# Three layer norms inside their layers' blocks, and a first group of keys stacked in two halves

## The reference

```python
x = x + attn(_layernorm(x))     # L0 bond attention, L1 selective scan, L2 dual attention, L3 plain attention
x = x + ffn(_layernorm(x))      # L0 masked, L1 experts, L2 ternary weights, L3 int8 weights

# L1 ffn: softmax over 128 logits, arg max chooses one of 8 experts, its output times the probability
# L2 ffn
h = silu((x @ w1.T) * s1) * ((x @ w2.T) * s2)
h = gelu((h @ h1.T) * sh1); h = gelu((h @ h2.T) * sh2)
out = (h @ w3.T) * s3
# L3 ffn, weights int32 times 1/127
out = (silu(x @ wg.T) * (x @ wu.T)) @ wd.T
# L2 attn (its dense half) and L3 attn: 16 heads of 8
out = softmax(q @ k.T * scale) @ v
```

## Time and profile before

| | us |
|---|---|
| median of three executions | 3002.31 |
| lowest, highest | 2993.35, 3003.5 |
| profiled execution | 3001.56 |
| its span, first to last instruction | 2999.8 |
| mean granted clock of TensorE | 0.906 of full |
| busy PE, ACT, DVE, POOL | 2391.6, 2010.3, 1861.0, 1070.1 |
| DMA, share of 16 engines | 16.3% |

### The profile page before, as it was taken

The page is one execution under the profiler, slowest core; times in us unless marked ns, Lnnn a source line. Parts: engine busy times, 40 slices in busy tenths (PEclk is TensorE's granted clock), DMA queues, the critical chain, the costliest instruction groups (busy, mean ns, idle before and its releaser), DMA issues. The chain is left out here.

```text
span 2999.8 us, 33172 instructions
## 1 busy us (share of the span) xinstructions
PE 2391.6 (80%) x12604; PEld 834.6 (28%) x12604; DVE 1861.0 (62%) x2715; ACT 2010.3 (67%) x2036; POOL 1070.1 (36%) x408
## 2 busy tenths in 40 slices
PE   3677787767666666767999889998679679999995
PEld 1122222334222222333222332223434412222223
DVE  5788888857999999865899438995330401102114
ACT  3999999813633333334999759996332379999991
POOL 4999999611099999431002200031000000000000
PEclk8899999978888898878999999999879879999997
DMA  2012211110154444103111100001010220210000
GB/s 74 1 43 59 69 43 43 43 53 8 29 182 160 168 159 156 58 13 82 30 26 21 41 1 11 11 3 45 7 40 0 53 46 17 42 30 14 15 7 27
DMA packets 66705, 144.64 MB, mean 48 GB/s; under 512 B 15115, under 2 KB 29799, under 8 KB 65832
## 3 DMA queue, kind: packets, MB, share of 16 engines
q1 hardware_dynamic: 66536, 142.40, 16.3%
HBM read 117.92 MB, written 24.25 MB: 47 GB/s over the span
## 5 line engine op out<-in xcount | busy, mean ns | idle before, releaser
L602 POOL TENSOR_TENSOR l0a_diff_pool<-l0a_A,l0a_a_of_t 128x2048 f32<-128x2048 f32 x128 | 531.7, 4192 | 36.3 <-ACT l0a_a_of_t L617 35.8
L1829 ACT ACTIVATE l2x_pT<-ps 128x1024 f32<-128x1024 f32 x512 | 495.8, 1021 | 13.2 <-PE ps L1788 11.3
L1829 ACT ACTIVATE l3he_pT<-ps 128x1024 f32<-128x1024 f32 x512 | 496.0, 1021 | 9.9 <-PE ps L1788 8.1
L1190 PE MATMUL ps<-l1s_hc,all_ident 128*128 128x512 f32 x512 | 285.1, 710 | 155.1 <-POOL l1s_hc L1161 100.7
L585 DVE SCALAR_TENSOR_TENSOR l0a_diff_dve<-l0a_A,l0a_pos,ps 128x512 f32<-128x512 f32 x512 | 345.0, 743 | 30.4 <-PE ps L460 30.4
L1152 POOL TENSOR_TENSOR l1s_dBx<-l1a_dtx,l1a_Bs 128x1024 f32<-128x1024 f32 x128 | 297.4, 2352 | 112.1 <-POOLq L886 112.1
L1176 ACT ACTIVATE ps<-l1a_dt,l1a_A 128x1024 f32<-128x1024 f32 x128 | 143.1, 1118 | 267.9 <-DVE l1s_hc L1235 215.7
L1788 PE MATMUL ps<-l3h_Qs,l3h_Ks 75*128 75x512 bf16 x1024 | 271.1, 389 | 24.7 <-DVE ps L1877 24.7
L1788 PE MATMUL ps<-l2m_Qs,l2m_Ks 75*128 75x512 bf16 x1024 | 273.5, 392 | 9.8 <-PEq L2111 9.8
L1802 PE MATMUL ps<-l2x_pT,l2m_Va 128*9 128x512 f32 x2048 | 271.6, 603 | 1.2 <-ACT l2x_pT L1829 1.2
L1802 PE MATMUL ps<-l3he_pT,l3h_Va 128*9 128x512 f32 x2048 | 270.9, 602 | 0.6 <-ACT l3he_pT L1829 0.6
(11 more groups left out here) (443 smaller groups left out, 3357.2 us busy)
## 6 DMA issues: line engine op xcount, KB each, us to landing
l1a_Bs<-l1a_bc SPq DMA_DIRECT2D x64, 512.0 KB, 3.6
l1s_Cs<-l1a_bc SPq DMA_DIRECT2D x64, 512.0 KB, 4.7
l0a_band_rows<-l0a_band SPq DMA_DIRECT2D x32, 512.0 KB, 5.3
l0a_band<-l0a_exps SPq DMA_DIRECT2D x16, 512.0 KB, 5.1
l2m_Ks<-l2m_parts SPq DMA_DIRECT2D x36, 128.0 KB
l2m_Qs<-l2m_parts SPq DMA_DIRECT2D x72, 64.0 KB
l3h_Ks<-l3h_parts SPq DMA_DIRECT2D x36, 128.0 KB
l3h_Qs<-l3h_parts SPq DMA_DIRECT2D x72, 64.0 KB
```

Source lines behind the costliest of these rows:

```text
L602: pool.tensor_tensor(out, window(s), atb[:, p % 2, :].unsqueeze(1).broadcast_to([P, 4, CH]), ALU.subtract).then_inc(diff_pool, 1)
L1190: mm = pe.matmul(g.ps[:, (4 + 2 * h + q) * CH:(5 + 2 * h + q) * CH], g.ident[:, :], hc[:, m % NHC, q * CH:(q + 1) * CH], start=(n == 0), s ...
L1829: act.activation(pT[:, turn % NPT, :], g.ps[:, slot * QC:(slot + 1) * QC], ACT.Exp).then_inc(expd, 1)
```

## The change

Three layer norms (ln3, ln5, ln7) become objects of a new class `LayerNorm`, whose parts are called at the head of each engine's list in the layer's own block; the block of their own is gone. PE transposes into banks 4 to 7. ACT copies quarter 0 after its fifth block and not after its eighth. SP no longer waits for the loads; PE (ln3, ln5) and DVE (ln5, ln7) do. Of DVE's six steps after the root three become two, so that five remain. In ln5 the four scale vectors are loaded as 16 rows of 128, transposed by PE in one instruction and copied by DVE, and PE waits for that copy before the second product. In ln7 DVE turns the weights into floats while ACT takes the root.

In `head_prepare` ACT's order becomes: squares and copies of k0, k1; squares of k2, k3; copies of q0, q1; squares of q0 to q3; copies of k2, k3; the root; copies of q2, q3. DVE splits k0, k1, q0, q1, k2, then the guard, then k3, q2, q3. SP stores k0 and k1 and, with early True, stacks the first 1024 columns of k after these two; then q0, q1, stacks q, stores k2, the guard, k3, q2, q3. The late half of the first group's keys is stacked at the start of the heads' block on a semaphore of its own, for which PE waits before the ninth key tile of the first segment. The small products of the norm's maximum go to bank 0 instead of banks 2 and 3.

```diff
+    def sync(self, sp):
+        self.n = self.load(sp, self.loads)
+    def tensor(self, pe):
+        for b in range(TB):
+            pe.wait_ge(self.norm[b % 2], b // 2 + 1)
+            mm = pe.transpose(self.g.ps[:, self.at + b * P:self.at + (b + 1) * P], self.xn[:, b, :], self.g.ident[:, :])
+            if b % 4 == 3:
+                mm.then_inc(self.turned, 1)
+    def copy(self, eng, fn, q):
+        eng.wait_ge(self.turned, q + 1)
+        fn(self.g.hT[:, q * CH:(q + 1) * CH], self.g.ps[:, self.at + q * CH:self.at + (q + 1) * CH]).then_inc(self.copied[q % 2], 1)
+    def scalar(self, act):
+        act.wait_ge(self.var_ready, 1)
+        act.activation(self.sd[:, :], self.ve[:, :], ACT.Sqrt).then_inc(self.std_ready, 1)
+        act.wait_ge(self.scale_ready, 1)
+        for b in range(1, TB, 2):
+            act.activation(self.xn[:, b, :], self.g.X[:, b, :], ACT.Identity, bias=self.nm[:, b:b + 1], scale=self.rs[:, b:b + 1]).then_inc(self.norm[1], 1)
+            if b == 9:
+                self.copy(act, act.copy, 0)
+        self.copy(act, act.copy, 2)
+    def vector(self, dve, meanwhile=None):
+        step = Steps(dve, self.steps)
+        ve, sd, rs, tmp = self.ve, self.sd, self.rs, self.tmp
+        for b in range(TB):
+            last = dve.bn_stats(self.st[:, b, :], self.g.X[:, b, :])
+        step(last)
+        for b in range(TB):
+            last = dve.bn_aggr(self.mv[:, b, :], self.st[:, b, :])
+        step(last)
+        dve.tensor_scalar(ve[:, :], self.mv[:, :, 1], 1.0e-5, None, ALU.add).then_inc(self.var_ready, 1)
+        if meanwhile is not None:
+            meanwhile()
+        dve.wait_ge(self.var_ready, 1)
+        dve.wait_ge(self.std_ready, 1)
+        step(dve.reciprocal(rs[:, :], sd[:, :]))
+        step(dve.tensor_tensor(tmp[:, :], rs[:, :], rs[:, :], ALU.mult))
+        step(dve.scalar_tensor_tensor(tmp[:, :], tmp[:, :], -0.5, ve[:, :], ALU.mult, ALU.mult))
+        step(dve.scalar_tensor_tensor(rs[:, :], tmp[:, :], 1.5, rs[:, :], ALU.add, ALU.mult))
+        dve.scalar_tensor_tensor(self.nm[:, :], self.mv[:, :, 0], -1.0, rs[:, :], ALU.mult, ALU.mult).then_inc(self.scale_ready, 1)
+        for b in range(0, TB, 2):
+            dve.tensor_scalar(self.xn[:, b, :], self.g.X[:, b, :], self.mv[:, b, 0:1], rs[:, b:b + 1], ALU.subtract, ALU.mult).then_inc(self.norm[0], 1)
+        for q in range(1, NCH, 2):
+            self.copy(dve, dve.tensor_copy, q)
...
-        layernorm_transpose(nc, g, "ln3", load)
+        ln = LayerNorm(nc, g, ctx, "ln3", load, 4)
...
+            @block.sync
+            def _(sp):
+                ln.sync(sp)
...
             def _(pe):
+                ln.tensor(pe)
+                ln.loaded(pe)
 
                 def logits(q):
+                    ln.quarter(pe, q)
...
                 def experts(b):
                     if b >= 2:
                         pe.wait_ge(zrd[b % 2], b // 2)
+                    else:
+                        for q in range(2 * b + 2):
+                            ln.quarter(pe, q)
...
             def _(act):
...
             @block.vector
             def _(dve):
+                ln.vector(dve)
...
-    def stack_k(sp, hg, slot, sem):
...
-        rows_of(sp, 1, hg, Ks[:, slot, :, :], slice(0, T), sem)
...
+    def stack_k(sp, hg, slot, sem, cols=slice(0, T)):
...
+        rows_of(sp, 1, hg, Ks[:, slot, :, cols], cols, sem)
...
-        if not early:
+        if early:
+            stack_k(sp, 0, 0, hd.k_late, slice(T // 2, T))
...
+        COPIED = (0, 1, NCH, NCH + 1, 2, 3, NCH + 2, NCH + 3)
...
+        def copied(m):
+            return 2 * (COPIED.index(m) + 1)
...
+        def was_split(m):
+            return COPIED.index(m) + 1
...
 
                 def norms(n, at):
                     pe.wait_ge(squared, NCH * (n + 1))
-                    pe.wait_ge(qcp, 2 * (at + 1))
+                    pe.wait_ge(qcp, copied(at))
...
-                pe.wait_ge(qcp, 2 * 3)
-                pe.matmul(g.ps[0:1, 2 * CH:2 * CH + P], km[:, 0:1], g.ident[:, :], start=True, stop=True).then_inc(krow, 1)
+                pe.matmul(g.ps[0:1, 0:P], km[:, 0:1], g.ident[:, :], start=True, stop=True).then_inc(krow, 1)
...
-                pe.wait_ge(qcp, 2 * 4)
-                pe.matmul(g.ps[:, 3 * CH:3 * CH + 1], kr[:, 1:5, :].rearrange("a c s -> a (c s)"), g.ones[0:1, 0:1], start=True, stop=True).then_inc(kcol, 1)
+                pe.matmul(g.ps[:, 0:1], kr[:, 1:5, :].rearrange("a c s -> a (c s)"), g.ones[0:1, 0:1], start=True, stop=True).then_inc(kcol, 1)
                 norms(1, 1)
                 pe.wait_ge(qcp, 2 * HALF)
...
-                pe.matmul(g.ps[0:1, 2 * CH:2 * CH + P], km[:, 2:3], g.ident[:, :], start=True, stop=True).then_inc(urow, 1)
+                pe.matmul(g.ps[0:1, 0:P], km[:, 2:3], g.ident[:, :], start=True, stop=True).then_inc(urow, 1)
...
-                    if m >= NCH:
+                    if m == NCH:
                         act.wait_ge(nps, 1)
...
-                for m in range(NCH + 2):
+                for m in (0, 1):
                     square(m)
                     copies(m)
-                for m in (NCH + 2, NCH + 3):
+                for m in (2, 3):
                     square(m)
-                for m in (NCH + 2, NCH + 3):
+                for m in (NCH, NCH + 1):
+                    copies(m)
+                for m in range(NCH, HALF):
+                    square(m)
+                for m in (2, 3):
                     copies(m)
                 act.wait_ge(nps, 2)
                 act.wait_ge(kcd, 1)
                 act.activation(mT[:, :], bank(1), ACT.Sqrt, scale=km[:, 1:2]).then_inc(und, 1)
+                for m in (NCH + 2, NCH + 3):
+                    copies(m)
...
-                for m in range(NCH):
+                for m in (0, 1, NCH):
                     parts_of(m)
                 dve.wait_ge(nps, 1)
                 dve.tensor_reduce(km[:, 0:1], bank(0), AX, ALU.max).then_inc(kmd, 1)
-                parts_of(NCH)
+                parts_of(NCH + 1)
...
-                parts_of(NCH + 1)
...
+                dve.tensor_copy(km[:, 1:2], g.ps[:, 0:1]).then_inc(kcd, 1)
+                parts_of(2)
                 dve.wait_ge(und, 1)
...
                 dve.wait_ge(urow, 1)
...
+                parts_of(3)
...
                 def store(m, stored):
                     i, q = which(m)
-                    sp.wait_ge(split, m + 1)
+                    sp.wait_ge(split, was_split(m))
                     sp.dma_start(parts[i, :, :, q * CH:(q + 1) * CH].rearrange("a p t -> p a t"), pt[:, m, :, :]).then_inc(stored, 16)
-                for m in range(NCH):
-                    store(m, k_stored)
+                for m in (0, 1):
+                    store(m, k_stored[0])
...
-                    sp.wait_ge(k_stored, 16 * NCH)
-                    stack_k(sp, 0, 0, k_in[0])
+                    sp.wait_ge(k_stored[0], 32)
+                    stack_k(sp, 0, 0, k_in[0], slice(0, T // 2))
                 for m in (NCH, NCH + 1):
                     store(m, q_stored[0])
...
+                store(2, k_stored[1])
                 store_guard(sp, gsplit, gstored)
                 if early:
                     stack_guard(sp, 0, 0, q_in[0])
+                store(3, k_stored[1])
...
-                sp.wait_ge(k_stored, 16 * NCH)
-                sp.wait_ge(q_stored[0], 32)
-                sp.wait_ge(q_stored[1], 32)
+                for half in range(2):
+                    sp.wait_ge(k_stored[half], 32)
+                    sp.wait_ge(q_stored[half], 32)
...
+    if n == TB // 2 and j == 0 and hd.k_late is not None:
+        pe.wait_ge(hd.k_late, hd.KIN)
...
-                sp.dma_start(sc[:, i, :], I[f"L2_ffn_{nm}_s"].rearrange("(k p) -> p k", p=P), allow_slow_non_contiguous=True).then_inc(s, 16)
+                sp.dma_start(scr[K * i:K * (i + 1), :], I[f"L2_ffn_{nm}_s"].rearrange("(k p) -> k p", p=P)).then_inc(s, 16)
...
-        layernorm_transpose(nc, g, "ln5", load)
+        ln = LayerNorm(nc, g, ctx, "ln5", load, 4)
...
+                ln.tensor(pe)
+                ln.loaded(pe)
+                pe.transpose(g.ps[:, 3 * CH:3 * CH + 4 * K], scr[:, :], g.ident[0:4 * K, 0:4 * K]).then_inc(sct, 1)
                 for n in range(N1):
                     m, q = n % K, n // K
+                    if m == 0:
+                        ln.quarter(pe, q)
+                    if n == 1:
+                        pe.wait_ge(scc, 1)
...
+                ln.scalar(act)
+                act.wait_ge(scc, 1)
...
+                ln.vector(dve)
+                dve.wait_ge(sct, 1)
+                dve.tensor_copy(sc[:, :, :].rearrange("p i k -> p (i k)"), g.ps[:, 3 * CH:3 * CH + 4 * K]).then_inc(scc, 1)
+                dve.wait_ge(scc, 1)
+                ln.loaded(dve)
...
+                    if m == 0:
+                        ln.quarter(pe, q)
...
-                dve.tensor_scalar(w[:, :, :], wi[:, :, :], SCALE, None, ALU.mult).then_inc(deq, 1)
```

(7 more changed lines are left out.)

42 lines of the change are left out of this document (36 added, 6 removed).

## The result

The changed kernel takes 2982.17 us (median of five, 2980.09 to 2986.45) against 2999.01 for the kernel before (five, 2993.35 to 3003.5): a ratio of 0.9939, 95% interval 0.992 to 0.9957, by the ratio some 18 us less. The sign was right, the gain nearly twice the forecast one.

What follows compares the result with a forecast made beforehand. Five seams were taken as bound by chains of short steps, DMA landings or block ends, no engine full. From 3001.56 us, -1.1 -3.6 -1.4 -1.5 +4.4 -6.7 = -9.9 gave 2991.7 us, range 2983 to 3001.

Steps and rivals of the forecast that it cites:

- ln3's first product: Experts' layer norm: first logits matmul starts 1.1 us earlier, bounds 0.6 and 1.3.
- ln5's first product: Ternary layer's norm: first matmul starts 3.6 us earlier, bounds 2.5 and 4.1.
- ln7's first product: Last layer's norm: first matmul starts 1.4 us earlier, bounds 0.9 and 1.7.
- l2m: First dense attention's preparation, not stacked early: V late, three splits queued, block ends 4.4 us later, bounds 2.5 and 6.5.
- l3h: Second dense attention's preparation, stacked early: earlier start and half the bytes end the block 6.7 us earlier, bounds 4 and 9.3.
- The given-back part: Second attention's preparation, behind q stacking: K2's store (1.7 us) and three closing stores instead of two (0.9) lost again.
- the range's cap on the gain: Second attention's preparation: VectorE's drain would be done at 2404.5, which caps the gain at 9.3 us.
- The clock: PE's granted clock at the three norms' seams: 1.5 us gained, bounds 4 gained and 2 lost.
- (a): Rival, chance 0.2: best clock in ln5 and ln7, cheap V, second preparation limited by VectorE; -17.9, 2984 us.
- (b): Rival, chance 0.12: landings depend on fixed steps, not bytes, so halving gains only 1.0 in second preparation; 2997 us.
- (d): Rival, chance 0.06: the norms' fusion fails, PE waiting at loads or quarters; without its 7.6 us, 2999 us.
- (c): Rival, chance 0.07: V's late start costs 6.5 us in first preparation, all gain in second, ln3's clock lost; 3004 us.

Runs made afterwards that it cites:

- e8: Kernel before, unfused, with 18 extra PE transposes in ln5's norm and 8 in ln7's filling PE's idle gap; 2999.78 us, ratio 0.9983.
- e11: e4 with SyncE storing k3, q2, q3 before waiting for the guard's stores, and ln5's loads reordered; 2976.39 us, ratio 0.9911.
- e12: e11 with only the first 512 columns of the first group's keys stacked in the preparation; 2966.0 us, ratio 0.9871.
- e2: Kernel before with the changed preparation of both dense attentions and halved first keys, layer norms as before; 3000.08 us, ratio 0.9989.
- after: The changed kernel itself, in its first trace; 2982.17 us, ratio 0.9939.
- e3: Repeat of the changed kernel: the old l2m function was written down but not called; 2986.15 us, ratio 0.9936.
- e3b: Changed kernel with l2m prepared in the old order, l3h in the new; 2984.65 us, ratio 0.9933.
- e4: Changed kernel with VectorE's last three splits (k3, q2, q3) ahead of the wait for the guard's maximum, in both preparations; 2975.49 us, ratio 0.9906.
- e1: Changed kernel with both dense attentions' preparation as before, so only the three layer norms fused; 2992.59 us, ratio 0.9967.
- e14: e1 with e5's edits: fused norms and halved early keys, engine order in both preparations as before; 2984.46 us, ratio 0.9942.
- e5: Kernel before with only the halving: K's first half stacked after all four stores, the rest at the heads' start; 2990.37 us, ratio 0.9969.

## Why the prediction was wrong

| step | predicted | first trace | mean of traces |
|---|---|---|---|
| ln3's first product | -1.1 | -1.0 | -1.0 |
| ln5's first product | -3.6 | -3.4 | -2.6 |
| ln7's first product | -1.4 | -1.8 | -1.7 |
| rest of the stage behind ln3, ln5, ln7 (predicted as clock) | -1.5 | +2.5, -2.3, -1.9 | -1.9, -0.6, -1.2 |
| l2m | +4.4 | +4.6 | +4.5 |
| l3h | -6.7 | -9.8 | -14.2 |
| heads' clock | none | -3.4 | chance |
| code that is the same elsewhere | 0 | -2.9 | chance |
| sum | -9.9 | -19.4 | -18.7 |

The means: unfused against fused traces for the norms (e8 left out where its fillers act, e11 and e12 in ln5, whose loads they reorder); for l3h the four with all keys early in whole rows (52.3) against four with the change's code (e2, after, e3, e3b: 38.1). Their sum agrees with the ratios of the changed kernel and its repeat (18 and 19 us). Of the 9.5 us by which the first pair of traces exceeds the forecast, 6.3 lie in code that the change leaves alone: by that pair alone the miss would be mostly chance. The means leave that out and still come to -18.7, with most of the excess in l3h.

**The preparation of l3h is the step that failed**, in two terms. The first is "0.56 MB less at some 95 GB/s is 6 us": K's packets took 13.3 us in the trace of before and 5.1 after, 8.2 less, and the q stores are released 12.2 earlier, not 9.3: 3.5 by the earlier start, as predicted (3.6), and 8.7 by the shorter wait behind it (17.29 against 8.62), where 6 were predicted. The given-back part was right: from that release to the next block it was 14.1 us in the earlier trace rows and 16.5 here, 2.4 against 2.6 predicted. The second is the base, 47.2 us from a single trace with the stacking at its quick end; three others needed 18 us for the same packets. No row of that trace could show this, but the range's cap on the gain, 9.3, taken from the same trace's VectorE tail, treated 47.2 as fixed. As a limit on where the stage can end the cap held in the first trace (9.8 gained, the last split and its store ending the stage); as a limit on the gain it didn't, since the gain over the other traces of before is 14. In e4 the splits are early and the stage is no shorter, so SyncE's chain stands close behind that limit.

Some of the working doesn't add up either. 3.6 and 6 make 9.6 and not 9.3; the three closing stores are put at 1.2 and enter the sum as 0.9. Its 1.13 and 0.56 MB are 1.18 and 0.59 MB by the packets. "20 us after the first store instead of 25" doesn't follow from its own 9.3, which gives 16; it was 13.0 (2370.54 to 2383.52). Together these move the forecast by a few tenths. The late half was hidden, as predicted: in the changed kernel ScalarE is never idle for over 0.3 us behind its first eleven exponentials, and the ninth key tile comes at the 33rd.

**l2m was right** to the cause: V starts behind root and copies, VectorE idle 5.49 before the maximum ("some 4" was said), three splits behind it. V took 6.33 against 5.67, and half clock throughout (7.5) did not come: V ran at 0.50 for 5.3 us here and for 3.9 before. The Trainium skill's rule on idle gaps ("TensorE: Matmul & The Clock Gate", "HAM oscillation") would have made the stage's loss 6.5. The trace bears that out only in part: V did start at low clock, but the granted clock had fallen 5.0 us ahead of V, before the gap of 4.81 began, and in the kernel before V started at 0.50 behind a gap of 0.38.

**The norms** gave their first products as forecast in ln3, ln7 and in ln5 of the first trace. What failed in ln5 is the sentence that the 320 KB behind the h weights end by 2197.3: the last load held PE by 0.37 us in the first trace, but by 2.15, 2.95, 2.05, 1.77 and 2.37 in e1, e3, e3b, e4 and e14. **The clock** was taken as one guess of 1.5; e8 shows that filling the pause is worth some 2 us a stage. Taking the pause away doesn't bring that surely: in e1, e3 and e4 the load's wait in ln5 is a pause of its own, and the first product took 2.08 again; but it took 2.08 in e11 too, with no wait, and in e3 and e3b ln7's rest was 33.7 with no pause at all. ln3's loss in the first trace was a level that unfused traces show too (77.6). The 1.9 that the mean shows there isn't shown to be the clock: at either level the fused stage is 1.9 or 2.1 shorter, though the clock rises 5.4 us behind the first product at the long level (7.8 before) and 0.2 to 0.4 behind it at the short one (0.7 to 0.8 ahead of it before). What shortens it stays open.

**The rivals.** (a), 2984, came nearest, with ln5's and ln7's clock (-4.2) and VectorE's tail as it said, but not with a cheap V (+4.6 for its +2.5) and with ln3's +2.5 against it; that its sum was met all the same is the 6.3 us of chance. (b) and (d) fell by e5 and e1. (c)'s tail of over 12 us behind the splits didn't come: the last drain stands 5.4 behind them. The chance of 0.2 for (a) and the range's low end, 2983, were too tight on that side.

## What to carry to other kernels

A transfer issued early to gain time can hold the one that is needed next; here the gain in the second attention came from moving fewer bytes ahead of the stores, and none that could be told from the order that starts them sooner; a quarter was better than a half. Work that needs no answer belongs ahead of a wait and not behind it, on the engine that computes and on the queue that stores. Of a single pair of traces, compare stage by stage and ask of each whether code without the edit shows the same figure; here 12 us lay in stretches that nobody touched.

## What the runs showed of the hardware

- Row-wise stacking of 4 KB rows by DMAs of eight partitions took 13.3 us in one execution and 18 in three others of the same code (358 against 486 to 512 ns a packet) at the same DMA share of 0.5; 2 KB rows took 113 to 199 ns. The share agrees with the Trainium skill ("DMA: Bandwidth & Descriptors", "Why a DMA increments its semaphore by 16 and not by 1"), by which pieces of eight rows go over eight engines of sixteen.
- In the last layer's unfused stage the granted clock rose 2.2 to 2.5 us ahead of the first product in four traces. In the three in which PE paused for 1.93 or 1.94 us it was back at 0.50 about 1 us behind the product's start; in e8, with fillers and a pause of 1.18, it stayed at 1.00.
- The granted clock at the start of the heads is a matter of the execution. Windows of 8 us, e14 and e5, whose code is the same there (span, busy and counts of PE, PEld, DVE, ACT, POOL, then clock, share, GB/s):

```profile
2391.00:2399.00 8.00, 8.00 (x23) 1.78 (x21) 0.00 (x0) 6.21 (x7) 0.00 (x0) 0.50 0.55 88
2399.00:2407.00 8.00, 8.00 (x29) 1.25 (x32) 0.00 (x0) 4.58 (x6) 0.00 (x0) 0.50 0.55 83
```

```profile
2409.00:2417.00 8.00, 8.00 (x27) 1.85 (x29) 0.00 (x0) 6.32 (x7) 0.00 (x0) 0.56 0.56 86
2417.00:2425.00 8.00, 8.00 (x56) 1.71 (x48) 0.00 (x0) 7.97 (x10) 0.00 (x0) 1.00 0.55 77
```

  From the first exponential on, half clock lasts 16 us and more in the one and some 7 in the other, and the first 64 exponentials take 68.9 and 63.3.
